# Graph and attentions on one core: gather slots in six groups of three instead of three groups of four

## The reference, cut to what matters

```python
def _rgcn_conv(x, src, dst, etype, W, root, b):      # 1250 nodes, 768 columns, 8 relations, 41250 edges
    x_src = x[src]
    seg = dst * num_rel + etype
    sums = segment_sum(x_src, seg, num_nodes * num_rel)
    cnt = segment_sum(ones, seg)
    mean = (sums / maximum(cnt, 1)).reshape(num_nodes, num_rel, -1)
    return einsum('nri,rio->no', mean, W) + x @ root + b

xn = layernorm(x)
h = relu(_rgcn_conv(xn, ..., W1, root1, b1))
x = x + _rgcn_conv(h, ..., W2, root2, b2) + mix(xn)      # mix: an attention with random features
x = x + ffn(layernorm(x))                                # attention with routed low-rank experts
return x
```

## Time and profile before

| | |
|---|---|
| median of three runs | 3384.78 us (3378.73 to 3389.24) |
| profiled execution, first to last instruction (its span; no other time of it is given) | 3605.0 us |
| mean granted TensorE clock in it | 0.957 |
| gather part of layer 0, 630 to 1174 us | 544 us |
| gather part of layer 1, 1710 to 2257 us | 547 us |
| PE busy, whole span | 3193.7 us (89%) |

### The profile page before, as it was taken

The page is one execution under the profiler, slowest core; times in us unless marked ns, Lnnn a source line. Parts: engine busy times, 40 slices in busy tenths (PEclk is TensorE's granted clock), DMA queues, the critical chain, the costliest instruction groups (busy, mean ns, idle before and its releaser), DMA issues.

```text
span 3605.0 us, 61984 instructions
## 1 busy us (share of the span) xinstructions
PE 3193.7 (89%) x19397; PEld 2367.7 (66%) x19398; DVE 1792.2 (50%) x2967; ACT 782.7 (22%) x1113; POOL 1291.1 (36%) x1388
## 2 busy tenths in 40 slices
PE   6999999887787799999878878999987899998999
PEld 5788887665665688887666666676755555555555
DVE  6566666444444433333444544334367764556451
ACT  2211211000000312122000000444421345434540
POOL 2681112556555000001555555000042246533652
PEclk9999999989998999999988998999998899999999
DMA  4343344667677133233667767300032000000003
GB/s 142 104 135 118 115 143 132 225 227 251 225 229 232 50 105 113 97 113 115 228 214 237 243 228 227 108 13 26 13 107 70 19 18 18 1 18 18 18 13 104
DMA packets 101161, 433.83 MB, mean 120 GB/s; under 512 B 19648, under 2 KB 19971, under 8 KB 96818
## 3 DMA queue, kind: packets, MB, share of 16 engines
q0 software_dynamic: 55712, 266.87, 22.9%
q1 hardware_dynamic: 42593, 124.83, 11.0%
q10 hardware_dynamic: 2736, 40.50, 3.1%
HBM read 355.21 MB, written 76.88 MB: 120 GB/s over the span
## 4 chain that ended last, share of the span: by engine, by line
PE 64%; DVE 12%; DVEq 7%; issue 7%; another core or an unknown queue 6%; ACT 2%; POOL 1%; DMA 0%; POOLq 0%; ACTq 0%; SPq 0%
PE PS L1574 24%; PE PS L1704 12%; PE PS L1918 5%; PE PS L1737 3%; PE PS L1583 3%; PE PS L1849 2%; DVE NM L1495 2%; DVE HOT L1241 2%; DVEq L1241 2%; PE PS L1745 2%; PE PS L1901 2%; PE PS L1782 1%; PE PS L1902 1%; PE PS L1766 1%
## 5 line engine op out<-in xcount | busy, mean ns | idle before, releaser
L1574 PE MATMUL PS<-WHL,XT 128*125 (+1 forms) x3240 | 553.1, 330 | 13.3 <-DVE WHL L1002 4.2
L1574 PE MATMUL PS<-WHL,HT 128*125 (+1 forms) x3240 | 534.8, 327 | 8.6 <-DVE ROOT L1200 8.6
L1574 PEld LDWEIGHTS PS<-WHL,XT 128*125 128x125 f16 (+1 forms) x3240 | 442.0, 138 | 100.4 <-issue 12.4
L1574 PEld LDWEIGHTS PS<-WHL,HT 128*125 (+1 forms) x3240 | 443.1, 137 | 94.1 <-DVE ROOT L1200 9.0
L1223 DVE SCALAR_TENSOR_TENSOR ROOT<-PS,GS,ROOT x182 | 185.3, 1018 | 523.9 <-remote 257.4
L646 POOL TENSOR_TENSOR PL<-PF 125x500 bf16<-125x500 f32 (+1 forms) x360 | 322.3, 928 | 248.9 <-ACT PF L859 248.2
L1704 PE MATMUL PS<-GATB,HOT 128*125 128x384 f16 x1440 | 285.5, 358 | 94.7 <-DVE HOT L1241 68.3
L1241 DVE SCALAR_TENSOR_TENSOR HOT<-NODE,DSTF,WHLO (+1 forms) x720 | 297.4, 475 | 78.6 <-issue 69.7
L1084 DVE SCALAR_TENSOR_TENSOR MSG<-PS,MSG 125x768 f16<-125x768 f32 x160 | 153.0, 956 | 360.2 <-ACT MSG L685 358.7
L1704 PEld LDWEIGHTS PS<-GATB,HOT 128*125 x1440 | 212.6, 150 | 165.8 <-issue 118.7
L1704 PE MATMUL PS<-ROW,HOT 128*125 128x384 f16 x1392 | 265.4, 350 | 57.8 <-DVE HOT L1241 45.8
(11 more groups left out here) (291 smaller groups left out, 4444.3 us busy)
## 6 DMA issues: line engine op xcount, KB each, us to landing
msg_table<-MSG SPq DMA_DIRECT2D x160, 336.0 KB
WST<-in_wg_dram ACTq DMA_DIRECT2D x16, 2304.0 KB
WST<-in_wf_dram SPq DMA_DIRECT2D x7, 1536.0 KB
KROW<-key_rows POOLq DMA_DIRECT2D x54, 192.0 KB, 3.8
msg_table<-MSG SPq DMA_DIRECT2D x160, 39.0 KB
WST<-in_wm_dram SPq DMA_DIRECT2D x5, 1152.0 KB
GATB<-msg_table,SKEY POOLq DMA_INDIRECT x216
ROW<-msg_table,SKEY POOLq DMA_INDIRECT x216
```

The lines of the kernel that those rows point to most:

```text
L1574: ins = pe.matmul(PS[0:ROWS, b0 + h, 0:HALF], X[:, xp, k, bass.ts(t, ROWS)], panel_part(slot, wp, k, h), start=k == 0 and xp + wp == 0, st ...
```

## The change

The slots become 18, in six groups of three tiles: `AT` is 3 and `GSETS` 6, so a layer has 108 groups and 18 turns. `GATB`, `GATC` and a pad are replaced by one tile `GATA` with six slots; four slots stay in `ROW`, two in `MSG`, and the last six (`k >= STAGED` = 12) lie in `WST`, the weights' staging buffer. POOL waits, ahead of the first of those six, for `w_lo` of the panel that is in `WST` at that time. So that this comes early, the four steps on the next panel stand at root rows 0, 2, 3 and 4 instead of 1, 3, 5 and 7, and `weights_top` at 1 and 3. Both layers now have five root rows ahead and five inside, at turns 0, 3, 6, 9 and 12. The limits are still packed three groups to a number, so they are loaded twice in a turn of six groups.

Since `WST` is in use as gather slots, three loads start later: layer 1's second panel is loaded by ACT at the start of layer 1 instead of at the end of layer 0's messages; the mix attention's second panel is loaded by SP after layer 1 is done (`rows_done` 2) instead of before; and the bias of layer 1 after `rows_done` 1. The products themselves, their number for a tile and their order within a pass are the same. With the edges of this case a layer of the changed kernel has 108 groups and again nine that reach over a border.

```diff
-AT = 4
+AT = 3
-GSETS = 3
+GSETS = 6
+LPACK = 3
+TURNS = AG // GSETS
+STAGED = 4 * AT
-ROOT_AT = (((0, 5), (5, 6), (10, 7), (15, 8), (20, 9)), ((0, 3), (3, 4), (7, 5), (11, 6), (15, 7), (19, 8), (23, 9)))
+ROOT_AT = (((0, 5), (3, 6), (6, 7), (9, 8), (12, 9)), ((0, 5), (3, 6), (6, 7), (9, 8), (12, 9)))
...
-            return GATB[:, k, :] if k < AT else GATR[:, k - AT, :] if k < 2 * AT else MSG[:, k - 2 * AT, :] if k < 2 * AT + 2 else GATC[:, k - 2 * AT - 2, :]
+            return GATA[:, k, :] if k < 6 else GATR[:, k - 6, :] if k < 10 else MSG[:, k - 10, :] if k < STAGED else GATW[:, k - STAGED, :]
...
-                sp.wait_ge(*((S["bias_free"], 1) if L == 0 else (S["root_made"], RT)))
+                sp.wait_ge(*((S["bias_free"], 1) if L == 0 else (S["rows_done"], 1)))
...
             sp.wait_ge(S["w_lo"], W_MIX + 1)
+            sp.wait_ge(S["rows_done"], 2)
             sp.dma_start(WST[:, 0:WM], a["wm"][128:256, :]).then_inc(S["w_in"], 16)
-            sp.wait_ge(S["rows_done"], 2)
...
-                    if L == 0 and t == GSLOTS:
-                        edge_weights(0)
+                    if t == STAGED:
+                        if L == 0:
+                            edge_weights(0)
+                        g.wait_ge(S["w_lo"], (REL + 1) * (L + 1) + 1)
+                        g.sem_inc(S["pool_tick"], 1)
...
                     act.wait_ge(S["rows_done"], 1)
+                    load_panel(REL + 2)
                     relu(0)
...
                 if L == 0:
                     split_high(REL + 1, REL * RT + 1)
-                    load_panel(REL + 2)
-
-            split_high(W_MIX, ROW_SUMS + REL * RT + 1, WHM, WM)
+                else:
+                    split_high(W_MIX, ROW_SUMS + REL * RT + 1, WHM, WM)
...
-                    if t == 1:
+                    if t == 0:
                         panel_max(nq, ncols)
+                    elif t == 2:
+                        top_row(nq)
                     elif t == 3:
-                        top_row(nq)
-                    elif t == 5:
                         scales(nq)
-                    elif t == 7:
+                    elif t == 4:
                         split_low(nq, WHL if L == 0 else WHM, ncols)
...
                     with v.Fori(first, end) as i:
-                        limits = set_limits(v, i)
                         for gg in range(GSETS):
+                            if gg % LPACK == 0:
+                                limits = set_limits(v, i * (GSETS // LPACK) + gg // LPACK)
...
-                    if t == 3:
+                    if t == 1:
                         top_transpose((REL + 1) * (L + 1))
-                    elif t == 5:
+                    elif t == 3:
                         top_broadcast((REL + 1) * (L + 1))
...
-                                    pe.wait_ge(S[f"gat_in{slot}"], i * 16 + (16 * (AG // GSETS) * L + 16))
+                                    pe.wait_ge(S[f"gat_in{slot}"], i * 16 + (16 * TURNS * L + 16))
```

More of the change, by code:

```diff
@@ L99, in graph_and_attentions_kernel @@
         KEYF = sb(kctx, "KEYF", [128, TILES], bf16)
+        DSTG = sb(kctx, "DSTG", [AG, AT * 128], i32)
         kctx.close()
@@ L117, in graph_and_attentions_kernel @@
         GATR = ROWS4[:].bitcast(f16)
+        GATW = WST[:].bitcast(f16).rearrange("p (k c) -> p k c", c=2 * D)
         IDF = sb(top, "IDF", [128, 128], f32)
@@ L223, in graph_and_attentions_kernel @@
             hot1_made hot1_used cnt_done hir_made hir_out key_in0 key_in1 key_in2 key_in3 key_in4 keys_ready low_made relations_made relation_in inverse_made rows2_in keys_made counts_found counts_taken
-            hot_made gat_in0 gat_in1 gat_in2 gat_in3 gat_in4 gat_in5 gat_in6 gat_in7 gat_in8 gat_in9 gat_in10 gat_in11 pass_done pass_out group_used weights_made msg_hi rows_done
+            hot_made gat_in0 gat_in1 gat_in2 gat_in3 gat_in4 gat_in5 gat_in6 gat_in7 gat_in8 gat_in9 gat_in10 gat_in11 gat_in12 gat_in13 gat_in14 gat_in15 gat_in16 gat_in17 pass_done pass_out group_used weights_made msg_hi rows_done
             rows_top rows_row rows_all act_tick sp_tick pe_tick pool_tick relu_made h_scale h_t h_hi h_free gnn_out
@@ L321, in set_limits @@
         def set_limits(eng, i):
-            return eng.value_load(LIM[0:1, bass.ds(i, 1)], min_val=0, max_val=RT ** (2 * GSETS) - 1)
+            return eng.value_load(LIM[0:1, bass.ds(i, 1)], min_val=0, max_val=RT ** (2 * LPACK) - 1)
         def group_blocks(limits, gg):
-            both = limits // RT ** (2 * gg) % RT ** 2
+            both = limits // RT ** (2 * (gg % LPACK)) % RT ** 2
             return both // RT, both % RT + 1
         def gat_slot(k):
-            return GATB[:, k, :] if k < AT else GATR[:, k - AT, :] if k < 2 * AT else MSG[:, k - 2 * AT, :] if k < 2 * AT + 2 else GATC[:, k - 2 * AT - 2, :]
+            return GATA[:, k, :] if k < 6 else GATR[:, k - 6, :] if k < 10 else MSG[:, k - 10, :] if k < STAGED else GATW[:, k - STAGED, :]
         def join_rows(t):
@@ L1030, in block_limits @@
                 v.drain()
-                limits = GBT[:, 0:AG].rearrange("p (i g) -> p i g", g=GSETS)
+                limits = GBT[:, 0:AG].rearrange("p (i g) -> p i g", g=LPACK)
                 v.scalar_tensor_tensor(limits[:, :, 1], limits[:, :, 2], float(RT ** 2), limits[:, :, 1], ALU.mult, ALU.add)
@@ L1252, in _ @@
                     first = i + 1
-                passes(first, AG // GSETS)
+                passes(first, TURNS)
                 v.drain()
@@ L1691, in passes @@
                     with pe.Fori(first, end) as i:
-                        limits = set_limits(pe, i)
                         for gg in range(GSETS):
+                            if gg % LPACK == 0:
+                                limits = set_limits(pe, i * (GSETS // LPACK) + gg // LPACK)
                             lo, hi = group_blocks(limits, gg)
@@ L1718, in _ @@
                         ins.then_inc(S["pass_done"], 1)
-                    passes(i, ROOT_AT[L][n_ + 1][0] if n_ + 1 < len(ROOT_AT[L]) else AG // GSETS)
+                    passes(i, ROOT_AT[L][n_ + 1][0] if n_ + 1 < len(ROOT_AT[L]) else TURNS)
             pe.wait_ge(S["rows_done"], 2)
```

7 lines of the change are left out of this document (2 added, 5 removed).

## The result

The changed kernel takes 3332.89 us (median of 4 runs, 3326.95 to 3334.79), the kernel before 3385.77 (4 runs, 3378.73 to 3389.24): a ratio of 0.9842 [0.9828, 0.9856], 53 us faster. The direction was right; the gain is twice the 25 us of the prediction, and the time lies at the best end of the range, 3332 to 3412 us.

The account below looks back on a forecast made before the run. Waits, not a full engine, were taken to bound the gather parts, with POOL setting the pace. Layer 0 -24 and layer 1 -20 give -44; plus 10 for DVE and 9 for late completions: -25, 3360 us, range 3332 to 3412.

Parts of the forecast that it names:

- Late completions: Gather parts: passes whose end reaches DVE late, mostly taken as a profiling cost; 9 us allowed for those staying without a profile.
- DVE's unseen cost: DVE's work in the 234 passes: up to 0.2 us more each, 47 us at most; 10 us taken.
- The pace of PE and DVE in layer 1: Layer 1's gather part: passes, root rows and waits on PE and DVE need 410 us, against POOL's 397.
- the wait at a load of the limits: PE waits for DVE where limits are loaded: about 1 us for each of 36 threes, 1 us at each of four root rows.
- what follows: After PE's 0.66 us wait at a load of the limits: DVE's nearly full cycle raises it to about 1 us.
- No engine is full: In the two gather stretches neither PE nor POOL is busy throughout, so the waits decide.
- The base: Gather parts of the kernel before, spans less the chain's unknown share: 443 us in layer 0, 444 in layer 1.
- The removable waits: POOL's waits for slots in the gather parts, 28 us in layer 0 and 38 in layer 1, nearly all removable by more slots.
- Same: Rival: gather-part waits are small delays that more slots don't touch; -5 to +8 us, 3380 to 3393; chance 0.16.
- DVE's chain: Rival: addition and HOT rebuild in 234 passes become the limit; 3408 at 0.25 us extra; chance 0.25 together with late completions.
- The clock: Rival: each of 72 loads of the limits drops PE's clock, 1.7 us a time; 3463 us; chance 0.04.
- The late completions as a rival: Rival: lateness exists without a profile, 54 more passes cost 1.1 us each; 3402 us; chance 0.25 together with DVE's chain.

Follow-up runs that it names:

- e3: Changed kernel with one more VectorE operation (0.344 us) in each of the 234 passes, prompt chip: 3355.60 us, 22.7 more than the changed kernel.
- e1: The kernel before, unchanged, profiled again on a prompt chip: 3386.89 us, profiled span 3382.4.
- e5 to e17: The follow-up runs on late chips, where the kernel before takes 3594 to 3620 us: the changed kernel unchanged and variants of either kernel, 3474.10 to 3634.68 us.
- e18: Changed kernel with 27 slots in layer 0 and three slots of layer 1 filled before the split, prompt chip: 3327.18 us, ratio 0.9834.
- e9: The changed kernel, unchanged, on a late chip: 3621.36 us against 3614.77 for the kernel before, ratio 1.0009.
- e2: Changed kernel with POOL waiting for the group four back, so only 12 slots are filled ahead, prompt chip: 3357.61 us, ratio 0.9914.
- e4: Changed kernel with groups of four instead of three on the same 18 slots, prompt chip: 3333.32 us, ratio 0.9847.
- e17: Changed kernel without 102 of 324 gathers a layer (six slots of GATA after the first turn), late chip: 3474.10 us, ratio 0.9667.
- e16: Changed kernel with gathers of half a row, as many gathers with half the bytes, late chip: 3602.92 us, ratio 1.0029.
- e13: Changed kernel with groups of four on 18 slots (90 passes a layer) and layer 1's staged slots reordered, late chip: 3596.92 us, ratio 1.0004.
- e14: Changed kernel with 18 slots in three groups of six, 63 passes a layer, late chip: 3628.97 us, ratio 1.0095.

## Why the prediction was right in direction and wrong in size

By the two profiles of prompt chips, 3382.4 and 3331.8 us, the change brings 50.6 us:

- Layer 0, forecast 419 against 443, -24. Measured 409.8 and 0.5 for the later zero matmuls against 436.2: **-25.9**.
- Layer 1, forecast 424 against 444, -20. Measured 399.6 and 11.9 for two more root rows ahead (539.8 us between the parts instead of 527.9; forecast 12) against 439.3: **-27.8**.
- Late completions +9 and DVE's unseen cost +10. Measured **0 and 0**.
- The rest of the program: +3 us (1356.2 after the last pass, 1353.1 before; 1353.3 to 1355.9 in the other prompt runs of changed kernels). Not forecast, cause not sought.

**The step that failed most is the pair of allowances.** Of the 26 us between the forecast and these traces they are 19; the gather parts are 10, less 3 for the rest of the program. The 10 us for DVE's unseen cost were taken "near the lower end" of 0 to 47; e3's rows show the cycle of 2.78 us that the rows of four tiles gave (3.11 to 3.18 with the 0.34 added), nothing or little on top. The 9 us for late completions rest on the reading "I take them for a cost of profiling". That reading is false: e1, profiled, has none, and e5 to e17 are as slow without a profile as with one. They go with the chip, as far as these runs show. Taking 216 us off fitted the chip of the result, but the logic of what is left was wrong: there is no small remainder. On a late chip it is all there, and the gain is gone. That the times ahead of the prediction and of the result came from the prompt kind was luck for the direction; nothing in the prediction foresaw it.

**The pace of PE and DVE in layer 1 (the prediction calls it a clock) was put at 410 us, measured at most 399.6.** The term that was mis-sized is the wait at a load of the limits. The prediction took 1 us for each of 36 loads a layer and 4 us for the root rows. The changed kernel's layer 1:

```profile
PE PS L1712 <- DVE HOT L1248: 21.6, 31, 1.5
```

31 waits of 0.70 us, 21.6 us in all: the 0.66 that the chain 3.6 less 2.95 gave, without "what follows". That is 18 us less than 36 + 4; PE's busy time (375.7 us instead of 345 + 24) takes 7 of it back, and other waits 2. POOL, put at 397 in layer 1 and 411 in layer 0, is right to a few us: restart to last gather 395.9 and 401.2, with 2.5 us before and 2.4 after the zero matmuls and the 6 us at the end, 399.6 and 409.8. "No engine is full" ends here with two paces that lie on each other: in e18 POOL has less to do and PE's stands at 400.

**The base was 11 us too long, and this hid half of the error in the parts after.** 443 and 444 by taking off the chain's unknown share, 436.2 and 439.3 measured: the chain names only part of what late completions cost. In e9 it names 2.9% and 4.2% of the gather parts, 16 and 23 us, of the 140 us that each is longer. The parts after, 419 and 424 with their fronts, were 410.3 and 411.5, so 8.7 and 12.5 us too long; less the 6.8 and 4.7 us of the base, only 1.9 and 7.8 us of this show in the gains. That -24 stands so near -25.9 in layer 0 is two errors that cancel. The removable waits come out as 21 and 33 us (436.2 less 415, 439.3 less 406), not 28 and 38.

**Slots.** That more slots let POOL run is right (e2: 24.7 us). That they alone do is not: e2, with twelve, already has 29 us from smaller groups and the early panel together, where the prediction gave the end of the waits to the slots. With 18 slots e4 shows that the groups' size doesn't matter. The early restart, half of the slots' part, was in the sum (2 after instead of 5.8, 3 before).

**The rivals.** "Same" is excluded on prompt chips, and is what late chips give, for another reason. DVE's chain exists and has the price that was said, 0.17 us a pass in e3, but the changed kernel stays on the right side of it. The clock: the granted clock of the gather parts is 1.00 with waits of 0.7 us at every third group. It falls to the lower level once, in layer 0 just after the 2.01 us wait ahead of the first pass, and the 36 matmuls that follow take 7.74 us where later ones take 6.01. On a late chip it is 0.90; there PE's 50 waits for `HOT` in layer 0 last 2.2 us in the mean, the longest 4.6. The Trainium skill's rule cited ahead (page "TensorE: Matmul & The Clock Gate", section "HAM oscillation — how this bites in real kernels") does not reach waits of 0.7 us; for the long ones the trace agrees. The late completions as a rival come true on late chips, at 0 us of gain where the prediction gave 17 us of loss, and with another law.

The expectation that the profiled span "may rise to 3650 or more" failed here (3331.8), and on a late chip too (3609.6, against 3605.0 before).

## What to carry to other kernels

When a profile is hundreds of microseconds longer than the runs, profile again before building on it: the two may come from different chips, and a share "of an unknown queue" need not be the profiler's, nor the whole of what it stands for. When the paces of two engines lie within a few per cent of each other, compute both from their rows and add no allowance for what the rows do not show. What more buffers bring ends where the other engine's pace stands, and a smaller group or an earlier step may have brought part of it already; look at that other engine next (here PE's wait at the load of the limits, 22 us a layer).

## What the runs showed of the hardware

- Two kinds of chips for one program: 3384 to 3387 us on two, 3594 to 3620 on four, with the whole difference in the stretches with indirect gathers. On the latter `pass_done` comes late (100 of 182 passes by more than 0.5 us in the trace of before, and a pass is added up to 8.0 us after its last matmul), though the transfers are as fast (a packet of 6144 bytes takes 0.30 us against 0.29 in the mean).
- The lateness follows the gathers: with two thirds of them 55% of it is left (e17), with half the bytes all of it (e16), and with 90 and 63 passes instead of 117 between 63% and all of it, by the measure taken (e13, e14).
- POOL issues a gather every 1.25 us where nothing holds it up (0.95 and 0.30 us), whether 12, 18 or 27 may be open. In the changed kernel that is 300 to 307 GB/s at a DMA share of 0.88 to 0.90, and PE waits less than 3 us a layer for landings.
